# Mixture of experts: GpSimd adds two of the eight token tiles of each expert's output, and the outputs get a third buffer

## The reference

```python
router_logits = x2d @ gate_w
routing_weights = jax.nn.softmax(router_logits, axis=-1)
routing_weights, selected_experts = jax.lax.top_k(routing_weights, TOP_K)        # TOP_K = 8 of 64
routing_weights = routing_weights / jnp.sum(routing_weights, axis=-1, keepdims=True)
...
layer_w0 = ragged_dot(sorted_inputs, gate_k, ...)        # 256 -> 96, bfloat16
layer_w1 = ragged_dot(sorted_inputs, up_k, ...)
intermediate = jax.nn.silu(layer_w0) * layer_w1
expert_out = ragged_dot(intermediate, down_k, ...)       # 96 -> 256, bfloat16
out = jnp.einsum('tke,tk->te', unsorted, routing_weights)
return out.reshape(B, S, H).astype(jnp.bfloat16)
```

## Time and profile before

| | |
|---|---|
| time, median of 3 runs | 2390.32 us (2388.5 to 2397.09) |
| profiled execution, its own time | 2401.34 us |
| its span in the trace | 2399.2 us |
| granted TensorE clock, mean of the span | 0.857 of full speed |
| first to last start of an addition (L1280) | 592.5 to 941.4 us |

### The profile page before, as it was taken

How to read it: one execution, slowest core, us unless ns; L and a number is a source line. 1 busy time by engine, 2 the same in 40 slices (tenths; PEclk the granted TensorE clock), 3 DMA queues, 4 the chain that set the end, 5 groups by cost and what they waited for, 6 DMA issues and landing times. The chain is left out here.

```text
span 2399.2 us, 34791 instructions
## 1 busy us (share of the span) xinstructions
PE 1985.9 (83%) x11353; PEld 1305.1 (54%) x11353; DVE 1748.1 (73%) x3892; ACT 1344.8 (56%) x2644; POOL 422.0 (18%) x587
## 2 busy tenths in 40 slices
PE   6999999986777675885877996598999999958978
PEld 4776767664333333562753353465667676723545
DVE  6888888777999998756996874666636464668734
ACT  5777777765898887355444365423333333253641
POOL 2333333321111110101732000300101010110000
PEclk8999999997776876795678798599999999977989
DMA  6000000002212100502503100150000000042010
GB/s 225 1 4 1 4 1 4 1 1 100 57 43 60 60 1 23 161 3 43 108 2 80 48 3 18 51 203 2 2 2 1 1 1 1 1 121 67 16 37 18
DMA packets 62030, 94.52 MB, mean 39 GB/s; under 512 B 9403, under 2 KB 48139, under 8 KB 59415
## 3 DMA queue, kind: packets, MB, share of 16 engines
q1 hardware_dynamic: 58604, 87.81, 12.0%
q0 software_dynamic: 1728, 4.22, 0.8%
q10 hardware_dynamic: 1536, 0.49, 0.1%
HBM read 80.53 MB, written 10.49 MB: 38 GB/s over the span
## 5 line engine op out<-in xcount | busy, mean ns | idle before, releaser
L1280 DVE SCALAR_TENSOR_TENSOR moe_acc<-moee_eo,moe_wsel,moe_acc 128x256 f32<-128x256 bf16 x512 | 226.4, 512 | 0.6
L887 DVE SCALAR_TENSOR_TENSOR l_acc<-l_px,l0w_chan,l_acc 128x253 f32<-128x253 f32 (+2 forms) x288 | 137.5, 477 | 80.6 <-POOL l_acc L855 80.1
L1185 PE MATMUL moee_po<-moee_db,moee_hb 96*128 96x256 bf16 (+1 forms) x768 | 137.2, 347 | 23.2 <-ACT moee_eo L1212 18.3
L1212 ACT CAST moee_eo<-moee_po 128x512 bf16<-128x512 f32 x256 | 133.2, 595 | 38.5 <-PE moee_po L1185 36.4
L1170 PE MATMUL moee_pu<-moe_xb,moee_wb 128*128 128x512 bf16 x192 | 71.9, 515 | 77.2 <-DVE moee_ub L1269 77.2
L1185 PEld LDWEIGHTS moee_po<-moee_db,moee_hb 96*128 96x128 bf16 (+1 forms) x768 | 92.3, 122 | 75.0 <-ACT moee_eo L1212 23.5
L1724 ACT ACTIVATE l3xa_ex<-l3xa_pS 128x512 f32<-128x512 f32 x128 | 74.1, 605 | 81.8 <-PE l3xa_pS L1637 77.4
L1724 ACT ACTIVATE l2a_ex<-l2a_pS 128x512 f32<-128x512 f32 x128 | 73.9, 605 | 80.1 <-PE l2a_pS L1637 75.6
L560 PE MATMUL l_pz<-xT,l0w_w_in 128*128 128x256 f32 x384 | 111.4, 413 | 2.5 <-DVE l_sz L935 2.5
L560 PE MATMUL l_px<-xT,l0w_w_in 128*128 128x256 f32 x384 | 103.5, 393 | 4.3 <-DVE l_acc L887 4.3
L3118 ACT COPY l3b_bc<-l3b_pbc 128x512 f32<-128x512 f32 x48 | 28.1, 586 | 137.1 <-PE l3b_pbc L3068 137.1
(11 more groups left out here) (624 smaller groups left out, 5548.7 us busy)
## 6 DMA issues: line engine op xcount, KB each, us to landing
moe_wf<-in_moe_up SPq DMA_DIRECT2D x48, 256.0 KB, 3.2
l3w_w_in<-in_l_w_in SPq DMA_DIRECT2D x1, 8224.0 KB, 26.1
m1b_bc<-bc_rows SPq DMA_DIRECT2D x16, 512.0 KB, 11.2
moe_df<-in_moe_down SPq DMA_DIRECT2D x48, 128.0 KB, 3.5
l_qs<-parts_q SPq DMA_DIRECT2D x36, 128.0 KB
l0w_w_in<-in_l_w_in SPq DMA_DIRECT2D x2, 1536.0 KB, 13.1
l0w_w_out<-in_l_w_out SPq DMA_DIRECT2D x1, 3072.0 KB
parts_q<-l_pieces SPq DMA_DIRECT2D x16, 192.0 KB, 2.3
```

What stands on the lines that cost most here:

```text
L887: nc.vector.scalar_tensor_tensor(out=a, in0=px[:, 0:S - (L0_CONV - 1 - c)], scalar=w, in1=a, op0=ALU.mult, op1=ALU.add).then_inc(tap_done, 1)
L1185: last = nc.tensor.matmul(po[:, t, :], hb[rows, j % H, t * P:(t + 1) * P], db[rows, j % H, :], start=(n == 0), stop=(n == len(parts) - 1))
L1212: nc.scalar.copy(eo[:, e % 2, 2 * q:2 * q + 2, :], po[:, 2 * q:2 * q + 2, :]).then_inc(o_read, 1)
L1280: last = nc.vector.scalar_tensor_tensor(out=acc[:, t, :], in0=eo[:, e % 2, t, :], scalar=wsel[:, t, e:e + 1], in1=acc[:, t, :], op0=ALU.mu ...
```

## The change

VectorE adds only the first six token tiles (`NV` = 6). Tiles 6 and 7 go to GpSimd, in two instructions for each expert: it multiplies the two tiles of `eo` (128x512) by the weights, spread over the 256 values, into a new float32 tile `prod`, waits for that on a semaphore (`weighed`), and adds `prod` to `acc[:, 6:8]`. Both stand in GpSimd's queue behind the cast of piece `i + 3`, in slot `i`, and begin when all four quarters of the expert are in `eo`. GpSimd first waits for the routing weights (`routed`). The clearing of `acc` now stands behind three casts in place of two.

`eo` has three buffers (`ER`) in place of two. ScalarE may write the buffer of expert `e` when both VectorE (`used`) and GpSimd (`used_p`) are done with expert `e - 3`. Its rounding of tiles 6 and 7 waits for GpSimd's last addition.

```diff
--- before.py
+++ after.py
@@ -1085,6 +1085,7 @@
 
         with Stage(nc, "moee") as st:
             R, H, U, LAG = MOE_RING, 9, MOE_N, 3
+            ER, NV = 3, 6
             LAST = MOE_E - 1
 
             def before(i):
@@ -1107,7 +1108,8 @@
             ex = st.sbuf("ex", [P, 4, TOK], BF16)
             lx = st.sbuf("lx", [P, 2, TOK])
             hb = st.sbuf("hb", [P, H, TOK], BF16)
-            eo = st.sbuf("eo", [P, 2, NT, D], BF16)
+            eo = st.sbuf("eo", [P, ER, NT, D], BF16)
+            prod = st.sbuf("prod", [P, NT - NV, D])
             accb = st.sbuf("accb", [P, NT, D], BF16)
             prob = st.sbuf("prob", [P, NT, MOE_E])
             rest = st.sbuf("rest", [P, NT, MOE_E])
@@ -1120,9 +1122,9 @@
             logits, v_chain, shifted, prob_done, xb_done, zeroed = st.sem(
                 "logits", "v_chain", "shifted", "prob_done", "xb_done", "zeroed")
             (cast, g_done, u_done, g_read, u_read, exp_done, one_plus, ln_done, inv_done, gated, h_done,
-             o_done, o_read, used, summed, rounded) = st.sem(
+             o_done, o_read, used, summed, rounded, routed, used_p, weighed) = st.sem(
                 "cast", "g_done", "u_done", "g_read", "u_read", "exp_done", "one_plus", "ln_done",
-                "inv_done", "gated", "h_done", "o_done", "o_read", "used", "summed", "rounded")
+                "inv_done", "gated", "h_done", "o_done", "o_read", "used", "summed", "rounded", "routed", "used_p", "weighed")
             with st.block() as block:
 
                 @block.sync
@@ -1144,12 +1146,28 @@
                         nc.gpsimd.tensor_copy(wb[:, i % R, :, :, :], wf[:, i % R, :, :, :])
                         nc.gpsimd.tensor_copy(db[:, i % H, :], df[:, i % R, :]).then_inc(cast, 1)
 
-                    AHEAD = 2
+                    AHEAD = 3
                     for i in range(AHEAD):
                         cast_weights(i)
                     nc.gpsimd.memset(acc[:, :, :], 0.0).then_inc(zeroed, 1)
-                    for i in range(AHEAD, U):
-                        cast_weights(i)
+                    for i in range(U + LAG):
+                        if i + AHEAD < U:
+                            cast_weights(i + AHEAD)
+                        if i == LAG:
+                            pool.wait_ge(zeroed, 1)
+                            pool.wait_ge(routed, 1)
+                        if i >= LAG:
+                            for e in experts(i - LAG):
+                                if e >= 1:
+                                    pool.wait_ge(used_p, e)
+                                pool.wait_ge(o_read, 4 * e + 4)
+                                nc.gpsimd.tensor_tensor(
+                                    prod[:, :, :], eo[:, e % ER, NV:NT, :],
+                                    wsel[:, NV:NT, e:e + 1].broadcast_to([P, NT - NV, D]), ALU.mult
+                                ).then_inc(weighed, 1)
+                                pool.wait_ge(weighed, e + 1)
+                                nc.gpsimd.tensor_tensor(acc[:, NV:NT, :], acc[:, NV:NT, :], prod[:, :, :], ALU.add
+                                                        ).then_inc(used_p, 1)
 
                 @block.tensor
                 def _(pe):
@@ -1205,11 +1223,12 @@
                                                  scale=-1.0).then_inc(exp_done, 1)
                         if i >= LAG:
                             for e in experts(i - LAG):
-                                if e >= 2:
-                                    act.wait_ge(used, e - 1)
+                                if e >= ER:
+                                    act.wait_ge(used, e - ER + 1)
+                                    act.wait_ge(used_p, e - ER + 1)
                                 for q in range(4):
                                     act.wait_ge(o_done, 4 * e + q + 1)
-                                    nc.scalar.copy(eo[:, e % 2, 2 * q:2 * q + 2, :],
+                                    nc.scalar.copy(eo[:, e % ER, 2 * q:2 * q + 2, :],
                                                    po[:, 2 * q:2 * q + 2, :]).then_inc(o_read, 1)
                         if 1 <= i <= U:
                             j = i - 1
@@ -1221,7 +1240,10 @@
                             nc.scalar.activation(ex[:, j % 4, :], lx[:, j % 2, :], ACT.Exp,
                                                  scale=-1.0).then_inc(inv_done, 1)
                     for t in range(NT):
-                        act.wait_ge(summed, t + 1)
+                        if t < NV:
+                            act.wait_ge(summed, t + 1)
+                        elif t == NV:
+                            act.wait_ge(used_p, MOE_E)
                         nc.scalar.copy(accb[:, t, :], acc[:, t, :]).then_inc(rounded, 1)
 
                 @block.vector
@@ -1256,7 +1278,9 @@
                             link(nc.vector.tensor_tensor(prob[:, :, :], prob[:, :, :], across(small[:, 3, :, None]),
                                                          ALU.mult))
                             link(nc.vector.tensor_scalar(rest[:, :, :], rest[:, :, :], 0.0, None, ALU.is_lt))
-                            link(nc.vector.tensor_tensor(wsel[:, :, :], prob[:, :, :], rest[:, :, :], ALU.mult))
+                            nc.vector.tensor_tensor(wsel[:, :, :], prob[:, :, :], rest[:, :, :], ALU.mult
+                                                    ).then_inc(routed, 1)
+                            dve.wait_ge(routed, 1)
                             dve.wait_ge(zeroed, 1)
 
                     for i in range(U + LAG):
@@ -1275,10 +1299,10 @@
                             for e in experts(i - LAG):
                                 if e >= 1:
                                     dve.wait_ge(used, e)
-                                for t in range(NT):
+                                for t in range(NV):
                                     dve.wait_ge(o_read, 4 * e + t // 2 + 1)
                                     last = nc.vector.scalar_tensor_tensor(
-                                        out=acc[:, t, :], in0=eo[:, e % 2, t, :], scalar=wsel[:, t, e:e + 1],
+                                        out=acc[:, t, :], in0=eo[:, e % ER, t, :], scalar=wsel[:, t, e:e + 1],
                                         in1=acc[:, t, :], op0=ALU.mult, op1=ALU.add)
                                     if e == LAST:
                                         last.then_inc(summed, 1)
```

## The result

The changed kernel takes 2438.32 us (median of 4 runs, 2430.59 to 2444.65) against 2393.69 (median of 4, 2388.5 to 2397.09). The ratio is 1.0187, 95% interval 1.0148 to 1.0226: 45 us slower, 35 to 54. The forecast was +39, 2430, counted from the median of the three executions known then, 2390.32; a fourth moved it to 2393.69. The profiled execution of the changed kernel took 2430.59 us, a span of 2428.7. It was the fastest of its four, while the profiled one of the kernel before (2401.34 us) was slower than all four of that kernel's, so the two spans differ by only 29.5; the stage itself shows the loss. From the first start of an addition to the last it takes 390.3 us in place of 348.9, +41.4.

A forecast was written before the change was run, and what follows sets the result against it. VectorE was taken to bound the addition stage. Delays from GpSimd's operations, less the additions removed, gave +2.4 us for each of 16 groups, +39; on the median 2390.3 that was rounded to 2430 us, range 2411 to 2472.

The forecast's parts named there:

- VectorE sets the pace: Expert-output addition stage: VectorE, busy 347.2 of 349.5 us, was taken as the bound, with TensorE late because of it.
- What is removed: VectorE's additions of tiles 6 and 7: 128 of 0.396 us each, 50.7 us, leave the path that sets the pace.
- The delay rule: Beside GpSimd, a blocked VectorE addition ends G + 0.13 us after the previous one, G being GpSimd's length; 1.00 us delay at 1.27.
- Length of the multiplication: GpSimd's new 128x512 multiplication was put at 1.27 us, from a float32 row of the same operation and shape.
- lengths named as a sign: In the profile after, GpSimd's new operations were to take 1.3 to 1.6 us each.
- How much L1269 hides: VectorE's 1.14 us copy of `pu` from PSUM, 48 times, hides at most one GpSimd operation each; 80 x 1.00 - 50.7 = +29 us.
- Where they fall: Delays per slot between copies of `pu`: 1.2 us with one expert, 3.2 with two; +2.4 us per four-expert group.
- signs of being wrong: Additions staying at 0.48 us beside GpSimd, a multiplication of 2 us or more, or one-expert slots of 5.96 us or less.
- The sum: Whole addition stage: +2.4 us for each of 16 four-expert groups, +39 us in all.
- Casts and ends at nothing: GpSimd's weight casts change nothing, later clearing of `acc` is harmless, and the last GpSimd pair counts 0, within 1 us.
- Rival 4: GpSimd's new operations do not hold VectorE; ScalarE then bounds at 19.8 us a group: -44 us, 2346; chance 0.06.
- The scan row: Scan L2181, read as two SBUF tiles, takes 2259 to 2291 ns beside GpSimd: the one line seeming to speak against blocking.

## Why the prediction was right, and where it was not

- **VectorE sets the pace.** Right, but by a hair. I read a busy share of 99% and stopped there. The other chain, 22.4 us in most groups once VectorE was relieved, was 0.1 us behind.
- **What is removed, 50.7 us.** Right: VectorE executes 128 instructions fewer, and the median of an addition stays at 0.478 us.
- **The delay rule.** Right in form and size, and to 0.02 us at the place shown: 1.01 us for the lone float32 addition of 1.27 us, 0.28 us from the end of one to the end of the other. The runs that took GpSimd's reads away, or put VectorE's input into PSUM, show the cause, where the prediction had only a coincidence in time.
- **Length of the multiplication.** Mis-sized: I took 1.27 us from the float32 row, and with a bfloat16 input it is 1.04. Its delay is then 0.77 in place of 1.00, 15 us less over 64. Of the lengths named as a sign, 1.3 to 1.6 us, only the addition's came (1.33 in the median, 1.11 for the multiplication).
- **How much L1269 hides.** Mis-sized the other way. I had 90 us paid after the hiding, out of 128. In the trace, the mean durations in the stage of additions, clamp, `hb` and `gb` products are 0.694, 0.838, 0.831 and 0.706 us, and 0.476, 0.416, 0.692 and 0.690 in the kernel before or alone. The delays are thus 384 x 0.218 + 45 x 0.422 + 46 x (0.139 + 0.016) = some 110 us. The records that have only a weight cast beside them hold 19 us of it (18.7 in the kernel before), those with one of the new operations beside them 91, of 64 x 1.77 = 113 possible. So 22 us were hidden and not 38.
- **Where they fall.** My picture of a steady slot was wrong. One-expert slots last 5.17 and 7.18 (or 5.65 and 6.69) in turn, where I had 6.4, and two-expert slots 11.6 or 13.3, where I had 12.2. Half of the one-expert slots thus meet one of my signs of being wrong, 5.96 or less; their mean, 6.2, was near. So was the mean of a group, 25.0 for 24.9.
- **The sum.** 91 - 50.7 = +40, and the stage shows +41.4. That it meets the +39 is luck in part: the multiplication was put 15 us too dear and the hiding some 16 us too large, and the two cancel.
- **Casts and ends at nothing.** Right within what can be told.
- **Rival 4, a gain of 44 us if nothing blocks.** Not the case, and its price was wrong. I had summed ScalarE's work (19.8 us a group) and not its idle time while it waits for TensorE's short products at the lower clock, which the earlier trace rows could not show, since they are of a slot with one expert. Measured, the kernel gains 10 us without GpSimd's operations and 5 us with operations that do not block. The sign of the forecast did not hang on it; a forecast of gain would have.
- **The scan row.** The prediction misread it. The scan L2181 does not read two SBUF tiles, for one of them lies in PSUM, as its allocation in the kernel shows:

```python
dBu = st.sbuf("dBu", [P, R, CH, S])
...
dA = st.psum("dA", [P, RD, CH, S])
```

So the row that seemed to speak against the rule agrees with it: one input in PSUM, 2259 to 2291 ns beside GpSimd, as the additions from PSUM. A scan that does read two SBUF tiles stands elsewhere in the trace of the kernel before: L996, with `ones` and `xn`. All four of them, then one alone and one beside a GpSimd addition:

```profile
L996 DVE TENSOR_TENSOR_SCAN xn<-ones,xn x4: 684/973/1001, 24.1 to 327.0; 48x256 f32<-48x256 f32 x4
```

```profile
24.09 0.68 DVE L996 TENSOR_TENSOR_SCAN xn<-ones,xn 48x256 f32<-48x256 f32 x1
...
206.36 0.73 POOL L872 TENSOR_TENSOR l_ssum<-l_ssum,l_sq 128x256 f32<-128x256 f32 x1 [1.55 <-ACT l_sq L762]
206.63 1.00 DVE L996 TENSOR_TENSOR_SCAN xn<-ones,xn 48x256 f32<-48x256 f32 x1
```

It takes 0.68 us alone and 0.95 to 1.00 in the three places with GpSimd beside it: the scan is held up too. There was no conflict to decide, and rival 4 had one reason less than the prediction gave it.

## What to carry to other kernels

Work that is moved to GpSimd from a busy VectorE has to be priced on VectorE: each GpSimd operation that reads SBUF costs a VectorE queue of two-SBUF-input operations its own length less some 0.27 us, unless it falls beside an operation that reads PSUM. (The 0.27 is measured for additions that follow each other every 0.396 us.) Here 0.79 us of additions were given away for up to 1.77 us of standing still. And before work is taken off a full engine, remove it altogether in one run: what the time does then is about the most that the change can give, and where it gives less than the sum, look for the second chain and shorten both at once.

## What the runs showed of the hardware

- GpSimd's multiplication with a bfloat16 and a broadcast float32 input, 128x512, takes 1.04 us at the least, its float32 addition of the same shape 1.26.
- GpSimd clearings (0.98 and 1.27 us, write only) beside VectorE additions with two SBUF inputs disturb neither (additions 468 to 486 ns, clearings 977 to 979 and 1271 to 1272). An addition with one input in PSUM is not disturbed by a GpSimd operation that reads two SBUF tiles (467 to 485 ns).
- L1296, one bfloat16 input of 1024 and the same tile as output in 0.41 us, is held up by reading GpSimd operations although it has only one input (up to 1482 ns). In the run with clearings it never came to stand beside one, so whether writes alone hold it up stays open.
- TensorE's 24 short products (32 rows, 256 columns) take 5.30 us where the granted clock is 0.50 and 4.42 us where it is 0.61 on average, back to back in both.
- The Trainium skill (SBUF — State Buffer, "Who interferes with whom") says of a VectorE operation with two SBUF inputs that GpSimd operations which only write leave it alone. The clearings agree (486 ns at most). The scan of the earlier trace rows is no exception to that section, since one of its inputs lies in PSUM.
- A scan over two SBUF tiles (48x256) takes 0.68 us alone and up to 1.00 beside a GpSimd addition of 0.73 us that reads SBUF.
